# Projection steps of an attention kernel in every second slot, and one turned token block eight slots later

## What is computed

```python
def _tc_rmsnorm(x, t, gw, gb, bw, bb):
    g = (t @ gw.T + gb)[:, None, :]
    b = (t @ bw.T + bb)[:, None, :]
    inv_rms = jax.lax.rsqrt(jnp.mean(x * x, axis=-1, keepdims=True) + EPS)
    return g * x * inv_rms + b

def _attention(x, Wq, Wk, Wv, Wo):
    q = (x @ Wq.T).reshape(B, L, H, dh)      # k and v likewise
    attn = jnp.einsum('blhd,bmhd->bhlm', q, k) / scale
    p = jax.nn.softmax(attn, axis=-1)
    o = jnp.einsum('bhlm,bmhd->blhd', p, v).reshape(B, L, D)
    return o @ Wo.T

def _swiglu(x, gate_w, hid_w, out_w):
    return jax.nn.silu(x @ gate_w.T) * (x @ hid_w.T) @ out_w.T

x1 = x + _attention(_tc_rmsnorm(x, t, g1w, g1b, b1w, b1b), Wq, Wk, Wv, Wo)
return x + (x1 + _swiglu(_tc_rmsnorm(x1, t, g2w, g2b, b2w, b2b), gate_w, hid_w, out_w))
```

## Time and profile before

| | |
|---|---|
| median of 3 runs | 2368.65 us (2367.02 to 2369.7) |
| the profiled execution | 2364.32 us, span 2362.4 us |
| PE busy | 2247.2 us, 95% of the span |
| PEld busy | 1569.1 us, 66% |
| DVE busy | 1650.0 us, 70% |
| ACT busy | 1283.7 us, 54% |
| POOL busy | 1368.4 us, 58% |
| mean granted TensorE clock | 0.991 |

### The profile page before, as it was taken

One profiled execution on the slowest core, in us unless ns is written; L12 is line 12 of the kernel. 1 busy time (PEld: TensorE's weight loads), 2 busy tenths in 40 slices (PEclk: granted clock), 3 DMA queues, 4 the chain that ended last, 5 costly groups with the idle time before them and its releaser, 6 DMA issues.

```text
span 2362.4 us, 37636 instructions
## 1 busy us (share of the span) xinstructions
PE 2247.2 (95%) x10848; PEld 1569.1 (66%) x10848; DVE 1650.0 (70%) x2723; ACT 1283.7 (54%) x2286; POOL 1368.4 (58%) x955
## 2 busy tenths in 40 slices
PE   5999989999989999899999889999999999999998
PEld 4655547555457555475554468888888788888887
DVE  4777745777736777546777478877887788778877
ACT  3367772567753667825666644363436343544354
POOL 0288881689952898915989746504660366036702
PEclk9999999999999999999999999999999999999999
DMA  6432212322132323132221331145114611363125
GB/s 194 147 97 61 79 46 94 91 75 65 59 104 51 99 53 90 32 112 70 61 54 32 116 135 54 48 152 204 56 34 135 228 58 36 117 201 109 40 89 179
DMA packets 96435, 221.79 MB, mean 94 GB/s; under 512 B 15712, under 2 KB 15712, under 8 KB 94560
## 3 DMA queue, kind: packets, MB, share of 16 engines
q1 hardware_dynamic: 95792, 212.93, 29.8%
q10 hardware_dynamic: 432, 6.29, 0.7%
HBM read 144.71 MB, written 24.12 MB: 71 GB/s over the span
## 4 chain that ended last, share of the span: by engine, by line
PE 75%; DVE 9%; issue 7%; ACT 5%; SPq 2%; DMA 2%; POOL 1%; DVEq 0%; ACTq 0%; POOLq 0%
PE bank L1876 26%; PE bank L1890 12%; PE bank L983 9%; PE bank L1107 8%; PE bank L1062 7%; PE bank L1168 6%; DVE pmax L807 3%; PE bank L1093 3%; PE bank L1072 2%; SPq L387 1%; ACT qk_hi L624 1%; POOL sums L546 1%; PE bank L1048 1%; ACT probs_up L708 1%; DVE ow L1696 1%
## 5 line engine op out<-in xcount | busy, mean ns | idle before, releaser
L807 DVE TENSOR_REDUCE pmax<-bank 128x1 f32<-128x512 f32 x1024 | 645.4, 683 | 177.0 <-PE bank L1062 171.0
L1062 PE MATMUL bank<-ks,qs 96*128 96x512 f32 x1024 | 421.1, 422 | 35.5 <-DVE pmax L807 33.9
L546 POOL TENSOR_TENSOR sums<-sums,probs_up 128x1024 f32<-128x1024 f32 x192 | 453.7, 2385 | 0.0
L1168 PE MATMUL bank<-qs,ks 128*128 128x512 f32 x1024 | 421.4, 416 | 15.6 <-ACT probs L708 9.0
L1890 PE MATMUL bank<-ow,aw 128*128 128x512 f32 x1536 | 360.5, 392 | 2.2 <-DVE ow L1696 2.0
L1876 PE MATMUL bank<-H_hi,wt_hi 128*128 128x512 f32 x896 | 350.4, 391 | 8.3 <-DVE H_lo L1731 8.3
L1876 PE MATMUL bank<-H_lo,wt_hi 128*128 128x512 f32 x896 | 349.8, 390 | 0.0
L1876 PE MATMUL bank<-H_hi,wt_lo 128*128 128x512 f32 x896 | 349.8, 390 | 0.0
L708 ACT ACTIVATE probs_up<-bank 128x512 f32<-128x512 f32 x512 | 282.5, 606 | 97.2 <-PE bank L1168 92.7
L708 ACT ACTIVATE probs<-bank 128x512 f32<-128x512 f32 x512 | 287.3, 602 | 81.4 <-PE bank L1168 80.1
L1890 PEld LDWEIGHTS bank<-ow,aw 128*128 128x128 f32 x1536 | 285.0, 188 | 64.7 <-issue 6.6
(11 more groups left out here) (184 smaller groups left out, 3614.7 us busy)
## 6 DMA issues: line engine op xcount, KB each, us to landing
raw<-in_gu_w SPq DMA_DIRECT2D x66, 512.0 KB, 3.6
wo_raw<-in_out_w SPq DMA_DIRECT2D x128, 256.0 KB, 2.8
qs<-qk_hi SPq DMA_DIRECT2D x256, 64.0 KB, 2.0
ks<-qk_hi SPq DMA_DIRECT2D x128, 128.0 KB, 2.4
x<-attn_out SPq DMA_DIRECT2D x10, 1024.0 KB, 8.9
x<-in_x SPq DMA_DIRECT2D x8, 1024.0 KB, 7.8
qs<-qk_lo SPq DMA_DIRECT2D x128, 64.0 KB, 2.0
ks<-qk_lo SPq DMA_DIRECT2D x64, 128.0 KB, 2.4
```

The source lines that it names most:

```text
L546: nc.gpsimd.tensor_tensor(total, first, probs_of(s, heads), ALU.add) \
L807: nc.vector.reduce_max(pmax[:, t, h, hf:hf + 1], mbank[n % MB][:], AX_X).then_inc(sq_done, 1)
L1062: nc.tensor.matmul(mbank[n % MB][:], qs[0:96, u % 3, h, t * P:(t + 1) * P], ks[0:96, u // 2 % 2, h, hf * QB:(hf + 1) * QB], start=True, st ...
L1168: nc.tensor.matmul(sbank[i % SB][:], ks[:, g % 2, h, s * P:(s + 1) * P], qs[:, u % 3, h, :], start=True, stop=True).then_inc(st_ready, 1)
```

## The change

The seam tile's four steps move from slots 0, 1, 2, 3 to slot 30 of the unit before and slots 0, 2, 4 (three Q tiles and two K tiles a batch; the K tile at the start of unit 0 stays at 0 to 3). The middle tile moves to slots 12, 14, 16, 18: from 12 to 15 in units 0 and 2, from 14 to 17 in units 1 and 3, from 9 to 12 in unit 4. The three tiles in units 6 and 7 stay (Q for the next batch from slot 8, K from 8 and 13). The turned block hT(0, 0), which may not overwrite what unit 4's Q still reads, moves in unit 4 from slot 15 to slot 23. Evictions and stacks follow each tile's last step. One line falls away, so line numbers after it are one lower in the changed kernel.

```diff
--- before.py
+++ after.py
@@ -32,16 +32,15 @@
 IN_V = {1: ("Q", 1), NT - 3: ("K", 2, 0), NT - 2: ("mT", 0)}
 UNIT = NS * GH
 
-Q_EVEN = {2: 12, 4: 9}
-PROJECTED = {("K", 2, 1): (0, 1), ("Q", 2): (12, 1)}
+PROJECTED = {("K", 2, 1): (0, 1), ("Q", 2): (12, 2)}
 for odd in (1, 3):
-    PROJECTED.update({("Q", odd + 2): (odd * UNIT, 1), ("K", odd + 3, 0): (odd * UNIT + 14, 1),
-                      ("K", odd + 3, 1): ((odd + 1) * UNIT, 1), ("Q", odd + 3): ((odd + 1) * UNIT + Q_EVEN[odd + 1], 1)})
-
-PROJECTED.update({("Q", NU - 1): (5 * UNIT, 1), ("Q", NU): (6 * UNIT + 8, 1), ("K", NU, 0): (7 * UNIT + 8, 1),
+    PROJECTED.update({("Q", odd + 2): (odd * UNIT - 2, 2), ("K", odd + 3, 0): (odd * UNIT + 12, 2),
+                      ("K", odd + 3, 1): ((odd + 1) * UNIT - 2, 2), ("Q", odd + 3): ((odd + 1) * UNIT + 12, 2)})
+
+PROJECTED.update({("Q", NU - 1): (5 * UNIT - 2, 2), ("Q", NU): (6 * UNIT + 8, 1), ("K", NU, 0): (7 * UNIT + 8, 1),
                   ("K", NU, 1): (7 * UNIT + 13, 1)})
 
-HT_AT = {(4, 15): (0, 0), (5, 8): (1, 0), (5, 12): (2, 0), (5, 16): (3, 0),
+HT_AT = {(4, 23): (0, 0), (5, 8): (1, 0), (5, 12): (2, 0), (5, 16): (3, 0),
          (7, 0): (0, 1), (7, 1): (1, 1), (7, 4): (2, 1), (7, 6): (3, 1)}
 SUMS_AT = {(5, 1): (0, 0), (1, 1): (1, 1)}
 MAXIMA_AT = (6, 3)
```

## The result

The changed kernel takes **2348.88 us** (median of 4 runs, 2346.93 to 2350.59) where the kernel before takes 2367.84 beside it: ratio 0.9915, 95% interval 0.9903 to 0.9927. Forecast: 2350. The profiled execution took 2346.93 us, its span 2345.1, 17.3 less than the 2362.4 of before.

A forecast was written before the change was run, and what follows sets the result against it. PE was taken to wait in slots 6 to 21 for banks while DVE stands behind ACT's qk_hi. Batch gains, less the turned block, of 4.8 (first, third), 4.3 and 4.4 sum to 18.3 us: 2368.65 - 18.3 = 2350, range 2342 to 2360.

The forecast's parts named there:

- the wait goes in front of a burst: Middle tile: DVE's wait for qk_hi stays, but slot 21's values and sums, 3.41 us, cover it.
- The cause is one instruction: Slots 6 to 21: DVE stands for ACT's qk_hi before qk_lo, 1.11 us idle in unit 2, with maxima queued behind.
- The rival in which the wait moves along: Burst fails to cover, slot 21 caught: 20 middle tiles give back some 0.65 us each; 2363, chance 0.14.
- Units 1 to 3: Slots 6 to 21 take 15.65 us each; first-batch gains 0.83, 1.24 and 0.83 us.
- Unit 4: Slots 6 to 21 fall to 15.65 us as in the other units, from 18.56 in the first batch.
- the 2.91: Forecast gain in us of unit 4's slots 6 to 21, first batch; 2.41 in the second, 1.54 in the last.
- Unit 0: Slots 6 to 21, DVE the bound: gain 0.7 us a batch, bounds 0 and 1.5.
- the bound of 1.5: Upper bound in us of unit 0's gain: PE's idle time there, 20.16 - 18.70.
- The turned block: Block at unit 4's slot 23, three batches: price 1.7 us each, bounds 0.6 and 3.2, no burst covering it.
- The seam: Seam tile at 30, 0, 2, 4: slots' sum stays 9.42 us, gain 0; rival that it blocks: 2380, chance 0.06.
- the bank's margins: Work bank at the seam: margin 0.57 us before slot 30's first step, 0.4 before slot 5's sums.
- Busy rows as the limit: Rival: only PE's idle time can be won, some 12 us in all; 2357, chance 0.12.

The follow-up runs named there:

- e4: Changed kernel with the five middle tiles' spaced steps two slots earlier (10, 12, 14, 16): 2364.82 us, ratio 0.9971 to the kernel before.
- e5: Kernel before with only DVE's qk_lo of the five middle tiles two slots later in DVE's order: 2361.57 us, ratio 0.9960.
- e9: Changed kernel with ACT's four scalings of x in unit 4 eight slots later: 2350.75 us, ratio 0.9910 to the kernel before.
- e2: Kernel before with only the seam tile moved to slots 30, 0, 2, 4: 2376.72 us, ratio 1.0024.
- e7: Changed kernel with unit 0's middle tile two slots later (14, 16, 18, 20): 2347.61 us, ratio 0.9899 to the kernel before.
- e3: Changed kernel with the middle tiles' steps in neighbouring slots ending at the same slot (15 to 18): 2350.98 us, ratio 0.9921 to the kernel before.
- e13: The kernel of e10 with ACT's squares of unit 6 two slots earlier as well: 2337.56 us, ratio 0.9866 to the kernel before.
- e10: Changed kernel with turned blocks in unit 5, later unit 0 middle tile, later unit 4 scalings, unit 6's Q tile at 12, 14, 16, 18: 2337.35 us, ratio 0.9871.

## Why the prediction was right, point by point

The sum was 18.3 us. Read slot by slot in the four batches of the two traces, the units' gains less the block's price are 4.6, 4.1, 4.6 and 5.0: 18.3, less 0.5 for the seams (20 of 0.02 to 0.03). One burst at a lower clock takes back 1.5; the parts outside the attention batches are 1.0 shorter, which makes 17.3. So the sum holds, but by luck in part: unit 4 fell short by 0.65 in three batches, and the surplus of slot 21, 0.13 a tile, happened to make up for most of it. The 1.0 is no more than what those parts differ by between two executions of one kernel (last section).

- **What bounds it; the wait goes in front of a burst (right).** DVE's stand stays (qk_lo begins 1.04 us after the last step's slot, 177.30 against 176.26; forecast 1.33), and PE's wait is gone. e4 brings the wait back by moving the stand two slots away from the burst, and e5 wins half to two thirds of the gain of units 1 and 2 by moving DVE's instruction alone. "The cause is one instruction" was too narrow for unit 2, where PE also waits 0.28 us for ACT (e5). The rival in which the wait moves along had its condition wrong: slot 21 is not caught, because its bank is ahead of qk_lo.
- **Units 1 to 3 (15.65; measured 15.51, 15.53, 15.50).** The surplus is slot 21: forecast with the 3.41 us of unit 2 before, it lasts 3.28 (177.19 to 180.47). POOL's margin was forecast at 1.1 us and is 1.0: its last sum ends at 178.49, the sums on PE start at 179.50.
- **Unit 4 (15.65; measured 16.31): the one term clearly mis-sized.** "Their slots are then alike" was false. The moved steps had covered something: ACT scales x there, 0.72 us each. PE and ACT of slots 9 to 11:

```profile
230.23 0.40 PE L1167 MATMUL bank<-qs,ks 128*128 128x512 f32 x1
...
231.00 0.51 PE L1167 MATMUL bank<-qs,ks 128*128 128x512 f32 x1
...
232.10 0.50 PE L1167 MATMUL bank<-qs,ks 128*128 128x512 f32 x1 [0.35 <-ACT probs_up L707]
```

```profile
229.75 0.71 ACT L583 ACTIVATE x<-x,inv 128x512 f32<-128x512 f32 x1
230.36 0.59 ACT L707 ACTIVATE probs<-bank 128x512 f32<-128x512 f32 x1
230.84 0.72 ACT L583 ACTIVATE x<-x,inv 128x512 f32<-128x512 f32 x1
```

  Slots 9 and 10 last 0.77 and 1.10 us. Before, each held a step and lasted about 1.16 anyway, and ACT was in time. e9 shows it: 0.8 us a batch, three batches. I had asked what covers the added steps, not what the removed steps had covered. Nor had I seen the DMA wait that e2 brought out; since I summed the new slots and not the old causes, its going was in the 2.91 without a name.
- **Unit 0 (0.7; measured 0.76).** The working held too: the second maximum of slot 21 waits for DVE,

```profile
112.92 0.50 PE L1061 MATMUL bank<-ks,qs 96*128 96x512 f32 x1 [0.82 <-DVE pmax L806]
```

  and with the tile two slots later the wait is gone (e7), so the bound of 1.5 given there could be passed: 0.76 + 0.96 = 1.72.
- **The turned block (1.7; measured 8.86 - 7.14 = 1.72).** As forecast, DVE idles ahead of hT_lo, 1.04 us where 1.2 was forecast, and no burst lies between it and slot 27:

```profile
248.11 0.69 DVE L792 TENSOR_TENSOR hT_lo<-bank,hT_hi 128x512 fp32r<-128x512 f32 x1 [1.04 <-ACT hT_hi L604]
```

- **The seam (0).** 9.44 to 9.45, within my 9.6; the bank's margins held, and 20 seams cost some 0.5 us in all. What the seam's delay could have cost lay in unit 4, behind the K stack's DMA (e2). I had looked at the Q stacks' readers and not at the next tile that needs the stack's source buffer.
- **Busy rows as the limit (fell).** PE's busy time fell by 11.0 us, 2247.2 to 2236.2, with the same instructions, and 17.3 us were won where the idle time alone gave 12. The rule of the Trainium skill (Perfetto Trace Analysis, Identifying the Most-Contended Engine), that matmul busy time measures badly how near TensorE is to its limit, agrees. The other rule of the Trainium skill (Perfetto Trace Analysis, Optimization Strategy), that a repeating gap can mean too few buffers, pointed to a cure that wasn't needed: three banks are still three, and another order closed the gap in units 1 to 3.

## What to carry to other kernels

An engine that works in order and must stand for another one needn't be freed: put its stand right ahead of a stretch in which nobody waits for its results. Here that was worth 0.7 us a tile in units 1 to 3 (e4), and the gap between the steps 0.1 (e3). Before a step is moved, list what it has been covering where it stands now (ACT's scalings here, 0.8 us) and who needs the buffers of the work that follows it (the K stack's landing); a half of a change that is free within the whole can cost by itself.

## What the hardware showed that I had not expected

Bursts of the same 16 values matmuls last 1.92 us or up to 3.6. Slot 5 of unit 7 in the changed kernel, second batch and third:

```profile
648.75 0.79 PE L1167 MATMUL bank<-qs,ks 128*128 128x512 f32 x1 [0.82 <-ACT probs L707]
649.47 3.14 PE L1106 MATMUL bank<-probs_up,v 128*32 128x512 f32 x16
```

```profile
973.81 0.51 PE L1167 MATMUL bank<-qs,ks 128*128 128x512 f32 x1 [0.81 <-ACT probs L707]
974.25 1.92 PE L1106 MATMUL bank<-probs_up,v 128*32 128x512 f32 x16
```

The granted clock (third number from the end) by stretches of the second batch, ahead of that slot, its first 0.75 us, the burst, and after; below, the stretch ahead of the slot in the third batch:

```profile
646.00:648.75 2.75, 0.94 (x5) 0.65 (x6) 1.20 (x2) 2.72 (x6) 2.75 (x2) 0.96 0.36 83
648.75:649.50 0.75, 0.75 (x5) 0.31 (x5) 0.18 (x1) 0.75 (x2) 0.75 (x1) 0.50 0.51 118
649.50:652.40 2.90, 2.90 (x17) 0.69 (x20) 0.69 (x1) 1.90 (x4) 0.15 (x1) 0.58 0.44 100
652.40:653.40 1.00, 1.00 (x13) 0.12 (x5) 0.00 (x0) 0.60 (x1) 0.00 (x0) 1.00 0.00 0
```

```profile
971.06:973.81 2.75, 0.94 (x5) 0.66 (x5) 1.20 (x2) 2.72 (x6) 2.75 (x2) 1.00 0.35 80
```

The clock stood at its lower level, 1.2 GHz (0.50, of 2.4), at the start of the slot, after a stretch in which PE had been busy 0.94 of 2.75 us. The third batch reaches that slot after the same gap (0.81 us of waiting right ahead of the slot, 0.82 in the second, and the same 0.94 of 2.75 us busy) and keeps the full clock, so the gap alone doesn't decide; what does stays open. The traces here have none to three such bursts; those at slot 5 of unit 7 and slot 29 of unit 4, which are most of them, cost 1.3 to 1.7 us each by the slots. They are one reason why e7 and e9, whose gains are plain in the slots, came out longer in total than expected: those traces have three. For e13 they are not, since its trace and e10's have one each; what its other runs lost was not seen in a trace.

Nor are they all of the spread. The four attention batches of the changed kernel's second trace last 264.92, 264.89, 264.94 and 252.77 us, those of its first 264.96, 266.47 (with the burst), 264.94 and 252.78. Yet the second trace is 1.2 us longer: the parts ahead of, between and behind the batches, which the moved steps don't touch, take 2.8 us more. Gains of 2 or 3 us in 2350 are read from slots, not from medians.
